# Expert rows gathered by slot tables from one-hot products, with part of the shared network and the numbering moved

## The chip, the cores and the metric

The kernel runs on one core of a Trainium2 chip. TensorE (PE) multiplies matrices, VectorE (DVE), ScalarE (ACT) and GpSimd (POOL) do elementwise work, SyncE (SP) issues most transfers. Each engine executes its own instructions in the order written, and semaphores tie the engines together. The metric is the device time of one execution in microseconds, as the median of several runs.

## The reference

Four blocks work in turn on `x`, 16 sequences of 128 tokens of 256 numbers (2048 tokens), each added to it behind a gate: a cross attention of 16 heads over all 2048 context rows, with numbers rounded to 8 bits; a mixture of 32 experts with a shared network; a WKV recurrence over each sequence; a mixture of 8 experts with a shared network. The change touches the second block:

```python
logits = x @ w_router
probs = jax.nn.softmax(logits.astype(jnp.float32), axis=-1)
w_topk, sel = jax.lax.top_k(probs, K)              # K = 4 of E = 32
...
pos = jnp.arange(T * K) - starts[sorted_e]
valid = pos < CAP                                   # CAP = 128 rows for each expert
buf = jnp.zeros((E, CAP + 1, Hq), x.dtype).at[sorted_e, dest].set(x[tok])
g = jnp.einsum('ech,ehf->ecf', buf, w_gate)         # 256 x 176
u = jnp.einsum('ech,ehf->ecf', buf, w_up)
y = jnp.einsum('ecf,efh->ech', jax.nn.silu(g) * u, w_down)
...
out = jnp.zeros((T, Hq), x.dtype).at[tok].add(gath * wv[:, None])
sh = jax.nn.silu(x @ sw_gate) * (x @ sw_up) @ sw_down   # 256 x 704
sh = jax.nn.sigmoid(x @ w_shared_gate) * sh
out = out + sh
```

A token's place within an expert is the number of earlier choices of that expert; places from 128 on are dropped.

## The kernel before

Tokens are handled as 16 tiles of 128, in NG = 4 groups of G = 4. The stages follow one another, with the head of each laid over the tail of the one before.

The attention (`attention_*`) fills about the first 750 us. In it SP writes zeros to the three tables of rows in device memory, one store of 512 rows with every fourth head (L433), beside the transposing transfers of the weights.

The front (`front_*`) comes next. For each group, DVE normalises the rows (`normalise`), PE turns them (`turn_rows`) and multiplies by the router (`router`, L1164), ACT copies the logits (L1232), DVE finds the four best experts, builds one-hot rows `hot` (L1306) and their sum `mask` (L1311) in `choose`, PE counts the places by products of the mask with a matrix of ones and a strictly triangular one (`places`, L1173 to L1177), and DVE's `place` (from L1318) turns counts into row numbers of the table `dispatched_rows` and closes the group with `destinations_ready`. `front_pool` then issues one indirect transfer for each tile and choice (L1142), 64 in all, each of which writes 128 rows (256 numbers, then the payload: experts, token numbers, weights) to their places in `dispatched_rows`. SP loads the shared weights and those of experts 0 to 9 (`load_expert`, L1048 to L1050; SLOTS = 10). The order of the work on each engine is written out by hand at the end of each `front_*` function.

The shared network is worked group by group. `hidden0(i, c0, c1)` is the hidden layer of group i in six chunks of 128 (the last of 64): PE makes the gate product (L1058, bank 0), ACT its silu (L1085), PE the up product (L1062, bank 1), and DVE multiplies them into `hT` (L1095). A gate product waits for the silu before, an up product for the multiplication before. `answers0(i)` is the down product of four tiles (L1075), each added to `x_sb` by DVE (L1103). Groups 0 and 1 stand at the end of the front, groups 2 and 3 in the mixing stage.

The experts (`experts_*`) follow. SP fetches the 128 rows of expert e from `dispatched_rows` (L1387) into one of RING = 6 buffers and loads the weights of expert e + 10 once expert e has been answered; PE turns the rows (L1409), multiplies by gate and up (L1418), turns the hidden layer (L1427) and multiplies by down (L1435), software-pipelined over three experts; ACT scales (L1457), takes silu (L1464) and weighs the answer into one of YRING = 4 buffers `yrow` (L1471); POOL scatters it to `answered_rows` by token and choice (L1529). DVE picks each row's target and weight out of the payload; `sum_payload(e)` (L1496) waits until the scatter of expert e - 4 has landed, and DVE's later work for e - 1 and e stands behind it.

The mixing stage (`mixing_*`) begins with the last expert. SP fetches the answered rows, and DVE adds them in `combine(g)` (L1959, then statistics L1946 and L1950). DVE's order begins: chunks 0 and 1 of group 2, `combine(0)`, chunks 2 and 3, `combine(1)`, chunks 4 and 5. PE's begins with all of `hidden0(2)` and `answers0(2)`. The second mixture, with its own tables and 39 blocks of rows (L2256 to L2283), ends the kernel.

## Time and profile before

| | |
|---|---|
| median of 3 runs | 1308.19 us (1306.60 to 1310.39) |
| the profiled execution, its own time | 1308.23 us |
| span of its trace, first to last instruction | 1306.4 us |
| busy: PE, DVE, ACT, POOL | 83%, 74%, 68%, 54% |
| attention | to about 750 us |
| front, groups 0 and 1 of the shared network | about 744 to 865 us |
| 32 experts | 865 to 961 us |
| mixing stage | 961 to 1179 us |
| second mixture | 1179 to 1306 us |

Times within the trace are microseconds from the start of its span. An engine's busy share over the whole span mixes stages with different limits, so each stage is read by itself: its windows, its waits, and the chain of work that ended last. PEclk is the granted TensorE clock as a share of 2.4 GHz.

### The profile page before, as it was taken

The page shows a single profiled execution, that of the slowest core. Times are in us where ns is not written, and L with a number is a line of the kernel's source. Part 1 is how long each engine was busy: PE and PEld are TensorE (multiplying, and loading weights), DVE is VectorE, ACT ScalarE, POOL GpSimd, SP SyncE. Part 2 cuts the span into 40 slices and gives each one's busy share as a digit, 9 for nine tenths or more (in the row PEclk, how much of TensorE's full clock was granted, in tenths as well). Part 3 has the DMA queues.
Part 4 walks back from the last instruction along what each step waited for, and adds up shares of the span by engine and source line. Part 5 has one row for each costly group of instructions (what it writes and reads, how often), then busy time and mean ns, then how long its engine had stood idle before and what let it go on. Part 6 is the DMA issues. An engine that isn't in the chain of part 4 may idle for free.

```text
span 1306.4 us, 23979 instructions
## 1 busy us (share of the span) xinstructions
PE 1086.5 (83%) x8185; PEld 634.8 (49%) x8300; DVE 962.8 (74%) x1787; ACT 893.6 (68%) x1533; POOL 702.6 (54%) x620
## 2 busy tenths in 40 slices
PE   6958888888888888888888768989988697798992
PEld 4623444444444444444444654556644254456771
DVE  6999899999999999999999564113345787642333
ACT  4649899999999999999999642124445466533441
POOL 3016988878888878887887437713330000452331
PEclk9969999999999999999999867989999898698997
DMA  5676788888888888888876391029853031123335
GB/s 172 126 140 140 152 171 160 162 175 166 166 184 160 160 181 166 167 180 163 161 149 106 58 278 60 19 58 275 257 190 133 1 82 51 42 83 92 100 95 208
DMA packets 393231, 182.50 MB, mean 140 GB/s; under 512 B 331376, under 2 KB 377045, under 8 KB 393112
## 3 DMA queue, kind: packets, MB, share of 16 engines
q1 hardware_dynamic: 384872, 164.30, 57.2%
q0 software_dynamic: 8016, 16.47, 3.6%
q8 instruction: 69, 1.13, 0.4%
q14 instruction: 50, 0.41, 0.1%
q10 hardware_dynamic: 224, 0.20, 0.1%
HBM read 52.70 MB, written 54.43 MB: 82 GB/s over the span
## 4 chain that ended last, share of the span: by engine, by line
PE 44%; DVE 31%; ACT 10%; issue 6%; DMA 5%; POOL 2%; SPq 1%; POOLq 0%; DVEq 0%; ACTq 0%
DVE top L368 20%; PE bank L217 8%; PE bank L231 7%; ACT weight L411 6%; PE bank L2267 4%; PE bank L1075 4%; PE bank L249 3%; DMA answered_rows<-yrow,target 3%; PE bank L1058 2%; PE bank L2283 2%; PE bank L1062 2%; PE bank L1435 2%; PE bank L1418 1%; PE bank L267 1%; DVE x_sb L1959 1%
## 5 line engine op out<-in xcount | busy, mean ns | idle before, releaser
L411 ACT ACTIVATE weight<-bank,bias,sq_all 128x1024 uint8<-128x1024 f32 x512 | 609.9, 1200 | 32.5 <-PE bank L231 27.1
L368 DVE TENSOR_REDUCE top<-bank 128x1 f32<-128x512 f32 (+1 forms) x683 | 610.8, 951 | 16.0 <-PE bank L217 4.7
L461 POOL CAST weight<-turned 128x2048 bf16<-128x2048 uint8 x256 | 478.8, 1892 | 43.5 <-PE bank L249 24.2
L231 PE MATMUL bank<-kT,query 128*128 128x512 bf16 x915 | 285.7, 384 | 26.3 <-ACT weight L411 12.1
L249 PEld LDWEIGHTS bank<-v_sb,weight 128*128 128x128 bf16 x4096 | 172.1, 97 | 109.8 <-POOL weight L461 7.5
L217 PE MATMUL bank<-kT,qspace 64*128 64x512 bf16 x687 | 138.2, 395 | 62.9 <-DVE top L368 62.9
L249 PE MATMUL bank<-v_sb,weight 128*128 128x16 bf16 x4096 | 172.7, 170 | 6.4 <-POOL weight L461 5.9
L217 PE MATMUL bank<-kT,query 128*128 128x512 bf16 x331 | 127.0, 384 | 2.1 <-DVE top L368 1.4
L1633 POOL DMA_INDIRECT dispatched_rows<-qspace,put x32 | 33.9, 1060 | 163.9 <-DVE qspace L2061 154.2
L231 PEld LDWEIGHTS bank<-kT,query 128*128 128x128 bf16 x1024 | 60.2, 97 | 104.2 <-ACT weight L411 60.9
L411 ACT ACTIVATION_READ_ACCUMULATOR weight<-bank,bias,sq_all 128x1 f32 x512 | 101.3, 198 | 0.0
L1142 POOL DMA_INDIRECT dispatched_rows<-qspace x64 | 64.0, 999 | 42.9 <-DVE qspace L1337 23.7
L217 PEld LDWEIGHTS bank<-kT,qspace 64*128 64x128 bf16 x687 | 33.4, 93 | 99.5 <-DVE top L368 94.3
L444 POOL TENSOR_TENSOR shift<-shift,nsq_all 128x4 f32<-128x4 f32 (+1 forms) x65 | 12.9, 198 | 127.9 <-DVE shift L372 127.9
L2388 POOL DMA_INDIRECT answered_rows<-yrow,target x39 | 37.9, 972 | 70.8 <-ACT yrow L2324 63.8
L1529 POOL DMA_INDIRECT answered_rows<-yrow,target x32 | 31.1, 972 | 81.2 <-ACT yrow L1471 76.4
L1085 ACT ACTIVATE sil<-bank 128x512 f32<-128x512 f32 (+1 forms) x24 | 14.3, 596 | 72.1 <-PE bank L1058 72.1
L217 PEld LDWEIGHTS bank<-kT,query 128*128 128x128 bf16 x337 | 32.7, 97 | 55.6 <-DVE top L368 36.4
L1058 PE MATMUL bank<-xT,sw 128*128 128x512 f32 (+1 forms) x96 | 49.3, 639 | 11.1 <-ACT sil L1085 10.3
L1095 DVE TENSOR_TENSOR hT<-sil,bank 128x512 f32<-128x512 f32 (+1 forms) x24 | 16.4, 682 | 57.2 <-PE bank L1062 49.4
L2359 DVE TENSOR_TENSOR eh<-esil,bank 128x176 f32<-128x176 f32 x39 | 13.2, 338 | 59.8 <-ACT esil L2317 59.8
L1062 PE MATMUL bank<-xT,sw 128*128 128x512 f32 (+1 forms) x96 | 47.4, 617 | 10.5 <-DVE hT L1095 10.5
(298 smaller groups left out, 1538.8 us busy)
## 6 DMA issues: line engine op xcount, KB each, us to landing
dispatched_rows<-zeros SPq DMA_DIRECT2D x32, 524.0 KB, 3.2
answered_rows<-zeros SPq DMA_DIRECT2D x16, 512.0 KB, 3.1
late<-answered_rows SPq DMA_DIRECT2D x16, 512.0 KB, 6.1
wgu<-in_L_ffn_w_gate SPq DMA_DIRECT2D x32, 176.0 KB
wgu<-in_L_ffn_w_up SPq DMA_DIRECT2D x32, 176.0 KB
wdn<-in_L_ffn_w_down SPq DMA_DIRECT2D x32, 176.0 KB
erow<-dispatched_rows SPq DMA_DIRECT2D x39, 131.0 KB, 2.1
dispatched_rows<-zeros SPq DMA_DIRECT2D x8, 536.0 KB, 3.1
```

The costliest lines, as they stand in the source:

```text
L217: pe.matmul(bank[:, k, :], q, kT[rows, h // 2, kb * 512:(kb + 1) * 512], start=True, stop=True).then_inc(s_blk, 1)
L231: mm = pe.matmul(unit[u % 2][:, v * 512:(v + 1) * 512], query2[:, t % 2, h, :], kT[:, h // 2, first + v * 512:first + (v + 1) * 512], star ...
L249: mm = pe.matmul(bank[:, 7, h * HD:(h + 1) * HD], weight[:, m % 3, r // 2, :, r % 2], v_sb[:, r, h * HD:(h + 1) * HD], start=(r == 0), sto ...
L368: ve.tensor_reduce(top[:, first:first + count], bank[:, first % 3:first % 3 + count, :], AX.X, ALU.max).then_inc(s_max, 1)
L411: ac.activation(weight8[:, n % BYTES, u * 1024:(u + 1) * 1024], unit[u], ACT.Exp, bias=bias[:, n:n + 1], scale=sq_all[:, n:n + 1], accum_o ...
L461: po.tensor_copy(weight[:, n % 3, :, :, :].rearrange("p c q two -> p (c q two)"), turned8[:, n % 3, :, :].rearrange("p c q -> p (c q)").bi ...
L1058: mm = pe.matmul(bank[0:w, 0, :], swg[:, k, c * P:c * P + w], xT[:, k, g * 512:(g + 1) * 512], start=k == 0, stop=k == CK - 1)
L1062: mm = pe.matmul(bank[0:w, 1, :], swu[:, k, c * P:c * P + w], xT[:, k, g * 512:(g + 1) * 512], start=k == 0, stop=k == CK - 1)
L1075: mm = pe.matmul(bank[:, 6 + k % 2, 0:C], hT[0:w, c, k * P:(k + 1) * P], swd[0:w, c, :], start=c == 0, stop=c == NW0 - 1)
L1142: po.indirect_dma_start(out=dispatched, out_offset=bass.IndirectOffsetOnAxis(ap=put[:, t, k:k + 1], axis=0), in_=rows0[:, t, :], in_offset ...
L2267: mm = pe.matmul(bank[:, 2 + b % 2, 0:2 * F1], erowT1[:, b % 2, k, :], w1gu[:, expert[b], k, :], start=k == 0, stop=k == CK - 1)
L2388: po.indirect_dma_start(out=answered1, out_offset=bass.IndirectOffsetOnAxis(ap=target1[:, b % YRING:b % YRING + 1], axis=0), in_=yrow1[:, ...
```

## The change

1. The 64 scatters are gone, and with them the table `dispatched_rows` and its zero stores (56 stores become 49 and a small one). SP instead stores each group's rows once, as they lie, to `kept_rows` (four stores). The remaining zero stores describe their table as partitions x 4 rows x row.
2. A table of sources is built: for each slot (0 to 127) of each expert, which row of `kept_rows` belongs there (row 0 to 127 of it are zeros). It comes from products of two one-hot arrays: `marked` (DVE, `mark_slots`, 128 x 16 x 128 in bf16: is this choice's place slot s?) and `numbered` (POOL, five `tensor_scalar` for each group: tile number and lane number at the chosen expert). PE's `fill_table(g)` adds 16 products for each group into bank 7; DVE's `take_table` turns the sums into row numbers. `marked` and `numbered` are single buffers, so that both wait for the products of the group before.
3. `place` loses two operations on 128 x 128 and a cast, and reads the counts from PSUM directly. `places` loses one product.
4. In the front, chunks 0, 1 and 2 of the shared network's group 0 are put between the routing steps, chunks 3 to 5 behind them.
5. Group 1 of the shared network moves to the head of the mixing stage, ahead of group 2; DVE does `combine(0)` between its hidden layer and its answers.
6. Expert rows are gathered by POOL with one indirect transfer for each expert, in the same queue as its scatters and six experts ahead. SP issues only weights.
7. SP loads three experts ahead of the routing and the other seven between the stores of the groups. The second mixture's fetches use other semaphores.

The diff, cut to its core:

```diff
@@ front_sync @@
-                for e in range(SLOTS):
+                for e in range(3):
                     load_expert(sp, e)
+                for g in range(NG):
+                    sp.wait_ge(sm_["destinations_ready"], g + 1)
+                    sp.dma_start(kept[P * (1 + g * G):P * (1 + (g + 1) * G), :].rearrange("(t p) c -> p t c", p=P),
+                                 rows0[:, g * G:(g + 1) * G, :]).then_inc(s_kept, 16)
+                    for e in range(3 + 2 * g, min(5 + 2 * g, SLOTS)):
+                        load_expert(sp, e)
@@ front_pool @@
-                    for t in tiles(g):
-                        for k in range(K0):
-                            po.indirect_dma_start(out=dispatched, ...).then_inc(s_scatter, 16)
+                    if g > 0:
+                        po.wait_ge(sm_["table_products"], g)
+                    for k in range(G):
+                        n = slice(k * K0, (k + 1) * K0)
+                        po.tensor_scalar(numbered[:, n, 0, :], hot[:, g % 2, n, :], float(g * G + k + 1), None, ALU.mult).then_inc(sm_["slots_numbered"], 1)
+                    po.tensor_scalar(numbered[:, :, 1, :], hot[:, g % 2, :, :], lane[:, 0:1], None, ALU.mult).then_inc(sm_["slots_numbered"], 1)
@@ front_tensor @@
+                def fill_table(g):
+                    pe.wait_ge(sm_["slots_numbered"], 4 + 5 * (g + 1))
+                    pe.wait_ge(sm_["slots_marked"], g + 1)
+                    if g == 0:
+                        pe.wait_ge(sm_["projections_added"], 2 * NG)
+                    for n in range(G * K0):
+                        mm = pe.matmul(bank[:, 7, 0:2 * E0], marked[:, n, :], numbered[:, n, :, :].rearrange("p a e -> p (a e)"),
+                                       start=g == 0 and n == 0, stop=g == NG - 1 and n == G * K0 - 1)
+                    mm.then_inc(sm_["table_products"], 1)
...
                 turn_rows(2)
+                pe.wait_ge(s_wf, 64)
+                hidden0(0, 0, 1)
                 places(1)
                 router(2)
                 turn_rows(3)
+                hidden0(0, 1, 2)
                 places(2)
+                fill_table(0)
                 router(3)
+                hidden0(0, 2, 3)
+                fill_table(1)
                 places(3)
-                pe.wait_ge(s_wf, 64)
-                hidden0(0, 0, 6)
+                fill_table(2)
+                fill_table(3)
+                hidden0(0, 3, 6)
+                pe.wait_ge(sm_["rows_chosen"], 1)
                 answers0(0)
-                hidden0(1, 0, 6)
-                answers0(1)
@@ front_scalar @@
                 copy_rows(2)
+                shared_scalar(ac, 0, 0, 1)
                 copy_logits(2)
                 exponentials(2)
                 copy_rows(3)
+                shared_scalar(ac, 0, 1, 2)
                 copy_logits(3)
                 exponentials(3)
+                shared_scalar(ac, 0, 2, 3)
                 residuals(3)
-                shared_scalar(ac, 0, 0, 6)
-                shared_scalar(ac, 1, 0, 6)
+                shared_scalar(ac, 0, 3, 6)
@@ front_vector @@
+                def mark_slots(g):
+                    if g == 0:
+                        ve.wait_ge(sm_["slots_numbered"], 4)
+                    else:
+                        ve.wait_ge(sm_["table_products"], g)
+                    at = slots[:, g * G * K0:(g + 1) * G * K0]
+                    ve.tensor_tensor(marked[:], slot_b[:].unsqueeze(1).broadcast_to([P, G * K0, P]),
+                                     at.unsqueeze(2).broadcast_to([P, G * K0, P]), ALU.is_equal).then_inc(sm_["slots_marked"], 1)
...
                 normalise(3)
+                mark_slots(0)
                 place(1)
+                hidden0(0, 0, 1)
                 choose(2)
+                mark_slots(1)
                 place(2)
+                hidden0(0, 1, 2)
                 choose(3)
+                mark_slots(2)
                 place(3)
-                hidden0(0, 0, 6)
+                mark_slots(3)
+                hidden0(0, 2, 5)
+                take_table()
+                hidden0(0, 5, 6)
                 answers0(0)
-                hidden0(1, 0, 6)
-                answers0(1)
@@ experts @@
-                def fetch_rows(sp, e):
+                def gather_rows(po, e):
...
+                    po.indirect_dma_start(out=erow[:, e % RING, :], out_offset=None, in_=kept,
+                                          in_offset=bass.IndirectOffsetOnAxis(ap=source[:, e:e + 1], axis=0), bounds_check=P + NTOK - 1,
+                                          oob_is_err=False).then_inc(s_er[e % RING], 16)
...
                 def experts_pool(po):
+                    po.wait_ge(s_kept, 16 * NG)
+                    po.wait_ge(s_zero, 16 * ZEROED)
+                    po.wait_ge(sm_["rows_chosen"], 1)
+                    for e in range(RING):
+                        gather_rows(po, e)
                     for e in range(E0):
+                        if e + RING < E0:
+                            gather_rows(po, e + RING)
                         po.wait_ge(sx_["targets_ready"], e + 1)
                         po.wait_ge(sx_["answers_weighted"], e + 1)
@@ mixing_tensor @@
                         pe.wait_ge(sx_["answers_weighted"], E0)
+                        for c in range(NW0):
+                            hidden0(1, c)
+                        for k in range(G):
+                            answers0(1, k)
                         for c in range(NW0):
                             hidden0(2, c)
@@ mixing_scalar @@
+                        shared_scalar(ac, 1, 0, NW0)
                         for c in range(4):
                             shared_scalar(ac, 2, c, c + 1)
@@ mixing_vector @@
+                        for c in range(NW0):
+                            hidden0(1, c)
+                        combine(0)
+                        for k in range(G):
+                            answers0(1, k)
                         hidden0(2, 0)
                         hidden0(2, 1)
-                        combine(0)
                         hidden0(2, 2)
                         hidden0(2, 3)
                         combine(1)
```

## Rows read from the trace of the kernel before

**Rows 1.** Windows: stretch, its length, busy us by engine, PEclk, DMA share, GB/s.

```profile
768.00:784.00 16.00, 6.11 (x33) 5.71 (x33) 13.32 (x65) 6.99 (x16) 12.47 (x12) 0.51 0.93 285
830.00:865.00 35.00, 33.87 (x100) 17.27 (x98) 6.29 (x11) 3.58 (x6) 16.46 (x17) 1.00 0.04 10
885.00:945.00 60.00, 54.98 (x243) 37.52 (x243) 19.35 (x102) 26.80 (x83) 19.43 (x20) 1.00 0.96 272
```

**Rows 2.** The chain that ended last, 784 to 890: start, us, what.

```profile
784.79 0.29 PE bank L1173
...
795.32 3.52 PE bank L1058 x4
...
818.94 12.00 PE bank L1075 x48
...
867.65 0.68 PE bank L1409 x2
```

**Rows 3.** Timeline of the routing, DVE and PE: start, us, instruction, idle before it.

```profile
775.30 1.03 DVE L1311 TENSOR_REDUCE qspace<-qspace 128x128 bf16<-128x512 f32 x1
...
776.72 1.43 DVE L1285 TENSOR_SCALAR qspace<-x_sb,rec,nm 128x256 f32<-128x256 f32 x4
...
778.08 0.28 DVE L1318 TENSOR_TENSOR qspace<-bank,limit 128x128 f32<-128x128 f32 x1
...
781.07 0.47 DVE L1293 MAX8 qspace<-qspace 128x8 f32<-128x32 f32 x4
```

**Rows 4.** Nearest prices: page's groups, groups by form, one line, then the timeline.

```profile
L461 POOL CAST weight<-turned 128x2048 bf16<-128x2048 uint8 x256 | 478.8, 1892 | 43.5 <-PE bank L249 24.2
...
L1959 DVE TENSOR_TENSOR x_sb<-x_sb,late 128x1024 f32<-128x1024 f32 x16 | 19.6, 1224 | 3.1 <-DMA late<-answered_rows 2.7
...
L1005 POOL TENSOR_SCALAR wp<-wp,vscale x2: 922/922/922, 87.2 to 88.1; 128x256 f32<-128x256 f32 x2
...
12.21 0.37 POOL L994 TENSOR_SCALAR token_f<-token_f 128x64 f32<-128x64 f32 x1
...
793.57 1.65 PE L1176 MATMUL bank<-qspace,every 128*128 128x128 bf16 x15
```

**Rows 5.** Timeline, two POOL casts beside DVE additions that end at 977.62.

```profile
975.14 2.48 DVE L1959 TENSOR_TENSOR x_sb<-x_sb,late 128x1024 f32<-128x1024 f32 x2
...
976.81 0.86 POOL L1617 CAST kind<-kind_i 128x8 f32<-128x8 uint32 x1
...
977.78 0.20 POOL L1619 CAST qspace<-place_i 128x32 f32<-128x32 uint32 x1
```

**Rows 6.** Timeline at the head of the mixing stage.

```profile
980.10 3.65 PE L1062 MATMUL bank<-xT,sw 128*128 128x512 f32 x4 [5.80 <-DVE hT L1095]
...
994.71 6.03 PE L1075 MATMUL bank<-sw,hT 128*128 128x256 f32 x24 [0.84 <-DVE hT L1095]
```

**Rows 7.** Timeline, first products of the experts.

```profile
869.02 2.71 PE L1418 MATMUL bank<-wgu,qspace 128*128 128x352 f32 x4 [0.29 <-ACT qspace L1457]
...
874.72 1.35 PE L1418 MATMUL bank<-wgu,qspace 128*128 128x352 f32 x4
```

**Rows 8.** Timeline of POOL's scatters, and one line's longest.

```profile
878.51 0.97 POOL L1529 DMA_INDIRECT answered_rows<-yrow,target  x1 [27.16 <-ACT yrow L1471]
...
881.00 0.97 POOL L1529 DMA_INDIRECT answered_rows<-yrow,target  x1 [1.52 <-ACT yrow L1471]
...
962.70 0.97 POOL L1529 DMA_INDIRECT answered_rows<-yrow,target  x1 [0.30 <-issue]
...
L1633 POOL DMA_INDIRECT dispatched_rows<-qspace,put x32: 972/972/2446, 1111.2 to 1175.9; - x32
```

**Rows 9.** Landing of indirect transfers: L1142 in 768 to 772, L1529 in 885 to 895.

```profile
DMA to landing us min/median/max: 5.6/5.8/6.0
...
DMA to landing us min/median/max: 6.1/6.1/6.1
```

**Rows 10.** DMA issues of the page: one of an expert's three loads of weights.

```profile
wgu<-in_L_ffn_w_gate SPq DMA_DIRECT2D x32, 176.0 KB
```

More of the change, by code:

```diff
@@ L46, in program @@
     ROW = C + 3 * K0
-    dispatched = nc.dram_tensor("dispatched_rows", [E0 * CAP, ROW], F32).ap()
+    kept = nc.dram_tensor("kept_rows", [P + NTOK, ROW], F32).ap()
     answered = nc.dram_tensor("answered_rows", [NTOK * K0, C], F32).ap()
@@ L53, in program @@
     answered1 = nc.dram_tensor("answered_rows_1", [NTOK * K1, C], F32).ap()
[L54 removed]
+    ZEROED = (NTOK * K0 + E1 * NTOK) // 512 + 1
     HUGE, TINY = 1e18, 2.0 ** -60
@@ L87, in program @@
         s_wp, s_g = sem("projection_weights_loaded"), sem("gates_loaded")
-        s_zero = sem("dispatched_rows_zeroed")
+        s_zero = sem("tables_zeroed")
         xr = x.rearrange("t p c -> p t c")
@@ L420, in attention_sync @@
             def attention_sync(sp):
-                stores = [(table, width, r) for table, width in ((dispatched, ROW), (answered, C), (dispatched1, ROW1))
-                          for r in range(table.shape[0] // 512)]
+                stores = [(table[512 * r:512 * (r + 1), :].rearrange("(p f) c -> p f c", p=P), width)
+                          for table, width in ((answered, C), (dispatched1, ROW1)) for r in range(table.shape[0] // 512)]
                 for n in range(NHEAD):
@@ L430, in attention_sync @@
                         pad_queries(sp, t + 1)
+                    if n == 8:
+                        sp.dma_start(kept[0:P, :], zeros[:, 0:ROW]).then_inc(s_zero, 16)
                     if n >= 8 and n % 4 == 0 and n // 4 - 2 < len(stores):
-                        table, width, r = stores[n // 4 - 2]
-                        sp.dma_start(table[512 * r:512 * (r + 1), :].rearrange("(p f) c -> p (f c)", p=P), zeros[:, 0:4 * width]).then_inc(s_zero, 16)
+                        cleared, width = stores[n // 4 - 2]
+                        sp.dma_start(cleared, zeros[:, 0:4 * width].rearrange("p (f c) -> p f c", f=4)).then_inc(s_zero, 16)
                     sp.wait_ge(s_exp, 2 * n + 2)
@@ L1039, in program, with rows1_fetched @@
             s_er = [sem(f"x0_rows_fetched_{s}") for s in range(RING)]
+            s_er1 = s_ew[0:RING]
+            def rows1_fetched(b):
+                weights = 48 * len(range(b % RING, E0, SLOTS))
+                return weights + 16 * (b // RING + 1)
             s_es = [sem(f"x0_answers_scattered_{s}") for s in range(YRING)]
@@ L1119, in program @@
             mask = carve(NT * E0 // 2).bitcast(BF16).rearrange("p (t e) -> p t e", e=E0)
-            ge, slot = carve(G * E0).rearrange("p (t e) -> p t e", e=E0), carve(2 * G * E0).rearrange("p (b t e) -> p b t e", b=2, e=E0)
-            destf, put = carve(NT * K0), carve(NT * K0).bitcast(U32).rearrange("p (t k) -> p t k", k=K0)
+            slots = carve(NT * K0 // 2).bitcast(BF16)
             total, share = carve(NT), carve(NT)
+            table = buffers(first_experts)
+            marked = late[:, 6, :].bitcast(BF16).rearrange("p (n s) -> p n s", s=P)
+            numbered = late[:, 7, 0:G * K0 * E0].bitcast(BF16).rearrange("p (n a e) -> p n a e", a=2, e=E0)
+            slot_b, slot_n, lane, lane_n = table("slot_b", [P, P], BF16), table("slot_n", [P, P], U32), table("lane", [P, 1]), table("lane_n", [P, 1], U32)
+            tile_f, source = table("tile_f", [P, E0]), table("source", [P, E0], U32)
             def front_sync(sp):
@@ L1172, in places @@
                     at = bank[:, 3, 0:G * E0]
-                    pe.matmul(at, every[:], number[:].unsqueeze(1).broadcast_to([P, G, E0]), start=True, stop=False)
+                    pe.matmul(at, before[:], mask[:, g * G:(g + 1) * G, :], start=True, stop=False)
                     for t in range(g * G + G - 1):
                         first = max(t + 1 - g * G, 0)
-                        pe.matmul(at[:, first * E0:], every[:], mask[:, t:t + 1, :].broadcast_to([P, G - first, E0]), start=False, stop=False)
-                    pe.matmul(at, before[:], mask[:, g * G:(g + 1) * G, :], start=False, stop=True).then_inc(sm_["places_counted"], 1)
+                        mm = pe.matmul(at[:, first * E0:], every[:], mask[:, t:t + 1, :].broadcast_to([P, G - first, E0]), start=False,
+                                       stop=t == g * G + G - 2)
+                    mm.then_inc(sm_["places_counted"], 1)
+                def fill_table(g):
[7 more added lines that the diff above has]
+                    mm.then_inc(sm_["table_products"], 1)
                 def hidden0(i, c0, c1):
@@ L1305, in choose @@
                     settle()
+                    if g >= 2:
+                        ve.wait_ge(sm_["slots_numbered"], 4 + 5 * (g - 1))
                     step(ve.tensor_tensor(hot[:, g % 2, :, :].rearrange("p (t k) e -> p t k e", k=K0),
@@ L1330, in place @@
                     step(ve.reciprocal(sgate[:, s], sgate[:, s]))
-                    step(ve.tensor_reduce(destf[:, g * G * K0:(g + 1) * G * K0], picked[:], AX.X, ALU.add))
+                    with nc.allow_low_precision(reason="whole numbers, compared with those below 128"):
+                        step(ve.tensor_reduce(slots[:, g * G * K0:(g + 1) * G * K0], picked[:], AX.X, ALU.add))
                     settle()
```

59 lines of the change are left out of this document (26 added, 33 removed).

## The prediction

> **What bounds the kernel now.** I read the windows by stage first. While groups are routed (768 to 784), PE is busy 6.1 of 16 us at the lower clock of 1.2 GHz and DVE 13.3: DVE's steps set the time, PE has room. From 830 to 865 PE is busy 33.9 of 35 us with group 1 of the shared network, at 2.4 GHz, and before that with group 0. From 885 to 945 the DMA engines are 96% busy at 272 GB/s [rows 1]. The chain of waits says the same: routing ends at 795.32 with the first chunk, the answers of group 0 start at 818.94, and the first expert's rows are turned at 867.65, right behind group 1 [rows 2]. POOL's 64 scatters are in none of these: they end before the shared network does. Removing them gives nothing by itself. What counts is when the experts can start, what each costs, and what the moved group costs later.
>
> **Routing and tables, worked on the axis of the trace before.** Without its two operations on 128 x 128 (0.28 us) and the cast, `place` takes 2.5 us instead of 3.0 (778.08 to the next `choose` at 781.07) [rows 3]. So the second mask, which ended at 776.33, is ready at 775.8, and the last `normalise` ends at 777.7 (776.72 + 1.43, less 0.5) [rows 3].
>
> Unseen before is the marking of slots, 128 x 2048 in bf16 with one operand repeated along the row. The nearest row is an addition of 128 x 1024 at 1.22 us [rows 4]; twice that, less one fixed part, is 2.3. The lower bound is 1.2, if bf16 goes at double rate. I take 2.3: the reduction into bf16 (1.03 us for 512 elements [rows 3]) shows no gain from the type. POOL's numbering is four operations of 128 elements and one of 512. From 0.37 us for 64 and 0.92 for 256 [rows 4] I get 0.55 each and 1.7, so 3.9 us for a group; the bounds are 2.0 (at the rate of the 1.89 us cast of 2048 [rows 4], with five fixed parts) and 5. Sixteen products of the table cost 1.6 us at 1.2 GHz by fifteen at 1.65 [rows 4], 0.9 at 2.4 GHz.
>
> Marking and numbering of one group are released together, by the products of the group before. A POOL cast of 8 elements took 0.86 us, to 977.67, while DVE's addition of two SBUF operands ran to 977.62; a larger one behind it took 0.20 [rows 5]. So I let them follow each other: 6.2 us, not 3.9. The Trainium skill says this too (SBUF — State Buffer, "SBUF: two separate sides"): a DVE operation with two SBUF inputs and a GpSimd operation that reads SBUF exclude each other for the whole instruction. It speaks against the numbering on GpSimd, and the row above agrees with it; without exclusion the sum below would be 4.6 us smaller.
>
> DVE in order from 777.7: mark 780.0, place 782.5, multiply chunk 0 (0.7) 783.2, choose (3.7, from 781.07 to the count at 784.79 [rows 2, 3]) 786.9. PE counts and fills table 0 to 788.7. DVE marks to 791.0, places to 793.5, multiplies chunk 1 to 794.2, chooses to 797.9. PE's up product of chunk 2 waits for that multiplication; with table 1 it ends at 797.1. ACT's three silus and their table loads fit between DVE's steps. Then the single buffers bind: POOL wakes in 0.6, mark and numbering take 6.2, so table 2 can start at 803.9 and ends at 805.5 (at 1.2 GHz, as the product behind an idle 5.8 us at 980.10 [rows 6]); DVE marks group 3 to 807.8, POOL numbers to 811.7, PE fills to 813.3. Three chunks are left. Six took from 795.32 to 818.94, the first slow [rows 2]: three take about 13.2 us, so the answers start at 826.5, not 818.94. They take 12.0, and the experts start 0.6 behind, at **839.1** against 867.65: **-28.5 us**. The three chunks moved into the routing hide about 10 us of PE work, and the table takes that and 7.6 more. The source table is ready near 821.5 and six gathers need 6 x 1.27 us of POOL and a landing, so they hide behind the answers. The stores of `kept_rows` (0.5 MB each, in 768 to 813) and the seven later weight loads land long before 839; the load that fills the DMA in 768 to 784 [rows 1] is only thinned.
>
> **Experts.** The fetch latency is already in that start. PE now comes from full work: the first products of a pair of experts took 2.7 and 2.5 us against 1.35 later [rows 7]; **-2.7 us**. POOL has two indirect transfers for each expert. Back to back one costs 0.97 + 0.30 [rows 8], so 2.54 for both, against the 2.49 at which experts follow one another when nothing waits (878.51, 881.00) [rows 8]. If POOL must wake for each answer, it is 0.8 + 0.97 + 0.30 + 0.97 = 3.04. But from 878.51 to 962.70 the 31 steps took 84.2 us, 2.72 each [rows 8], since in the busy stretch scatters land after 6.1 us [rows 9] and the ring of four holds DVE. A gather in the same queue could lengthen that. Against it: 1.28 us apart, as dense as gather and scatter will be, L1142's scatters landed in 5.6 to 6.0 us with the DMA as full [rows 9]. Bytes per expert stay (528 KB of weights [rows 10], 134 in, 131 out), and at 272 GB/s [rows 1] they need 2.9 us whoever issues them. I take **+1.0 us**, bounds -3 and +9 (3.04 for the 26 steps with a gather against their present share).
>
> **Mixing.** Group 1 comes first. PE starts at 961.45 as now; six chunks end by 983.6 (five at 3.44 and a first one behind ACT's table load). `combine(0)` takes 6.8 us (four additions of 1.22 [rows 4], then statistics), to 990.4; its rows landed long before. Answers run beside it, but the third waits for DVE's first addition: end 997.0. Chunks 0 to 3 of group 2 end at 1010.8, `combine(1)` runs 1011.5 to 1018.3, chunk 4's multiplication to 1019.0, chunk 5 to 1021.5. Now group 2's answers start at 994.71, after an idle 5.8 us that also cost a product at 3.65 instead of 1.88 [rows 6]. **+26.8 us** for 34 us of moved work. Behind this point every engine's order is the same and the fetches have more slack.
>
> **Other edits.** Seven fewer zero stores, in smaller pieces, lie beside a stretch that DVE bounds; new semaphores and a product less: 0, bounds -1 and +2.
>
> **Sum.** -28.5 - 2.7 + 1.0 + 26.8 = -3.4 us on the profiled execution's 1308.23 (span 1306.4), which is the median within 0.1: **1304.8 us**.
>
> **Rivals.**
> - The tables are quick: marking and numbering run side by side (4.6 less) and PE stays at 2.4 GHz or marking is at double rate: -8 to -14, at 1300 to 1294; worked as 1299. For it: PE has more work in the routing. Against it: [rows 5].
> - Slower: POOL becomes the bound of the experts. A gather, never seen here, may cost more than a scatter; the longest indirect transfer took 2.45 us [rows 8]. With the whole gather at 1.8 us, POOL needs 0.97 + 0.30 + 1.8 + 0.30 = 3.37 for each of 26 steps: 26 x 3.37 + 5 x 2.49 = 100.1 against 84.2, +16 in place of +1: 1320. At 1.3 us (2.87) it only cancels the gain; it turns to slower by 0.3% at about 1.5. Against it: the scatters of 1072 and 1024 bytes cost the same 0.97.
> - It doesn't do what it says: the interleaved chunks delay DVE's routing as much as they hide. The main case has this nearly so. If additionally POOL pays its waking (3.04) at each expert, 1311: no change.
>
> **How the numbers follow.** Main case 0.45, its own range 1301 to 1309; quick tables 0.25; nothing gained 0.13; POOL bound 0.17. The range 1293 to 1317 takes in the quick case and half of the slow one. About 0.3% (3.9 us) is what a measurement can tell: faster means below 1304.3, which is nearly half of the main case and the quick one, 0.46; slower, above 1312.1, 0.19; between them 0.35.
>
> **What would show it.** In the changed kernel: marking at 2.3 us, POOL's five operations at 3.9 us and stretched beside marking; two PE gaps of about 5 us ahead of tables 2 and 3; the answers of group 0 starting near 826 and the first turn of expert rows near 839; POOL's pairs 2.54 us apart and weighed answers 2.7 apart; scatters landing in about 6 us; answers of group 2 some 60 us behind the last expert instead of 33. Wrong would be: gathers over 1.3 us, a wait of PE for gathered rows, or an attention that ends elsewhere than before.

## The result, and the profile after

The changed kernel takes **1299.33 us** (median of 4 runs, 1298.18 to 1300.09) against 1308.57 for the kernel before on the same chip: a ratio of 0.9933, with a 95% interval of 0.9918 to 0.9949. It is faster by 0.67%. The forecast was 1304.8, in a range of 1293 to 1317. The profiled execution took 1299.77 us, with a span of 1298.0 where the kernel before had 1306.4.

The windows of the changed kernel, over the stretches of [rows 1]:

```profile
core 0: us, PE busy (x) PEld busy (x) DVE busy (x) ACT busy (x) POOL busy (x), PEclk, DMA share, GB/s
768.00:784.00 16.00, 10.44 (x43) 7.55 (x42) 13.36 (x59) 8.90 (x16) 2.65 (x4) 0.79 0.38 113
830.00:865.00 35.00, 32.98 (x150) 22.57 (x149) 10.60 (x53) 14.80 (x46) 16.92 (x17) 1.00 0.61 176
885.00:945.00 60.00, 56.76 (x219) 34.75 (x217) 16.79 (x80) 25.32 (x66) 28.14 (x30) 1.00 0.67 214
```

DVE is as busy in the routing as it was (13.4 of 16 us); PE went from 6.1 to 10.4, part of it at 2.4 GHz, and the DMA engines from full to 38%. From 836 on, where group 1 of the shared network stood, experts are at work. The chain of waits of the changed kernel has these pieces, where [rows 2] had 795.32, 818.94 and 867.65:

```profile
796.90 2.49 POOL late L1166
800.11 1.57 POOL late L1167
801.73 1.05 PE bank L1209 x16
802.93 2.56 POOL late L1166
...
807.40 1.57 POOL late L1167
809.02 1.04 PE bank L1209 x16
810.05 3.49 PE bank L1064 x4
...
823.17 11.98 PE bank L1081 x48
...
835.71 0.46 PE bank L1466 x2
...
924.83 1.88 PE bank L1492 x8
...
987.83 6.03 PE bank L1081 x24
```

From 796 to 810 the chain runs through POOL's numbering (L1166, L1167) and the table products (L1209). Then come the shared chunks, the answers of group 0 at 823.17, the first turn of expert rows at 835.71, the last down product at 924.83, and the answers of group 2 at 987.83. The account of the two spans:

| stage | before | after | difference | forecast |
|---|---|---|---|---|
| start to the first expert turn | 867.65 | 835.71 | -31.9 | -28.5 |
| first turn to the last weighed answer | 93.75 | 91.5 | -2.3 | -1.7 |
| from there to the answers of group 2 | 33.3 | 60.6 | +27.3 | +26.8 |
| the rest | 311.7 | 310.2 | -1.5 | 0 |
| span | 1306.4 | 1298.0 | -8.4 | -3.4 |

The attention ends at the same time in both. The last weighed answer ends at 961.40 and 927.21 us.

### The profile page after: what moved, and what is told of

The parts are those of the page before. It is cut to its first block, busy times and chain, and to the rows that moved or that the text cites. A ratio compares the mean times of both kernels' runs of the same rounds, so it can differ in the third digit from the quotient of the medians.

```text
span 1298.0 us, 24037 instructions
## 1 busy us (share of the span) xinstructions
PE 1081.6 (83%) x8245; PEld 631.3 (49%) x8360; DVE 969.6 (75%) x1781; ACT 899.4 (69%) x1537; POOL 696.8 (54%) x610
## 4 chain that ended last, share of the span: by engine, by line
PE 42%; DVE 31%; ACT 10%; issue 7%; DMA 5%; POOL 4%; SPq 1%; POOLq 0%; DVEq 0%; ACTq 0%
DVE top L368 20%; PE bank L217 7%; PE bank L231 7%; ACT weight L411 6%; PE bank L2340 4%; PE bank L1081 3%; DMA answered_rows<-yrow,target 3%; PE bank L249 3%; PE bank L1064 3%; PE bank L2356 2%; PE bank L1068 2%; PE bank L1721 1%; PE bank L267 1%; DVE x_sb L2028 1%; POOL weight L463 1%
## 5 line engine op out<-in xcount | busy, mean ns | idle before, releaser
L411 ACT ACTIVATE weight<-bank,bias,sq_all 128x1024 uint8<-128x1024 f32 x512 | 610.0, 1200 | 32.4 <-PE bank L231 27.2
L231 PEld LDWEIGHTS bank<-kT,query 128*128 128x128 bf16 x1024 | 60.1, 97 | 104.2 <-ACT weight L411 60.6
L2461 POOL DMA_INDIRECT answered_rows<-yrow,target x39 | 37.9, 972 | 69.5 <-ACT yrow L2397 54.9
L2340 PE MATMUL bank<-late,erowT 128*128 x156 | 53.8, 468 | 0.0
L1081 PE MATMUL bank<-sw,hT 128*128 128x256 f32 x192 | 47.9, 393 | 4.6 <-DVE hT L1101 2.5
L1068 PE MATMUL bank<-xT,sw 128*128 128x512 f32 (+1 forms) x96 | 45.6, 597 | 4.7 <-DVE hT L1101 4.7
```

The costliest lines, as they stand in the source:

```text
L231: mm = pe.matmul(unit[u % 2][:, v * 512:(v + 1) * 512], query2[:, t % 2, h, :], kT[:, h // 2, first + v * 512:first + (v + 1) * 512], star ...
L411: ac.activation(weight8[:, n % BYTES, u * 1024:(u + 1) * 1024], unit[u], ACT.Exp, bias=bias[:, n:n + 1], scale=sq_all[:, n:n + 1], accum_o ...
L1068: mm = pe.matmul(bank[0:w, 1, :], swu[:, k, c * P:c * P + w], xT[:, k, g * 512:(g + 1) * 512], start=k == 0, stop=k == CK - 1)
L1081: mm = pe.matmul(bank[:, 6 + k % 2, 0:C], hT[0:w, c, k * P:(k + 1) * P], swd[0:w, c, :], start=c == 0, stop=c == NW0 - 1)
L2340: mm = pe.matmul(bank[:, 2 + b % 2, 0:2 * F1], erowT1[:, b % 2, k, :], w1gu[:, expert[b], k, :], start=k == 0, stop=k == CK - 1)
L2461: po.indirect_dma_start(out=answered1, out_offset=bass.IndirectOffsetOnAxis(ap=target1[:, b % YRING:b % YRING + 1], axis=0), in_=yrow1[:, ...
```

## Experiments

Each ratio is to the kernel before on the same chip. Where the routing starts varies by up to 2 us between traces of these kernels; so, where it matters, times are counted from the start of the first marking (777.68 in the changed kernel, where chunk 3 starts 32.4 us later and the answers of group 0 45.5 later).

### Group 1 back in front of the experts

```diff
@@ front @@
                 answers0(0)
+                hidden0(1, 0, 6)
+                answers0(1)
@@ mixing_tensor @@
-                        for c in range(NW0):
-                            hidden0(1, c)
-                        for k in range(G):
-                            answers0(1, k)
```

> The changed kernel (1299.3 us, profiled span 1298.0) with group 1 of the shared network put back behind group 0, ahead of the experts; tables, gathers and interleaving stay. My theory: the front takes 33.9 us more (first expert turned near 869.6 instead of 835.7), the mixing stage's head 27.3 us less (group 2's answers 33.3 us behind the last expert instead of 60.6): 1299.3 + 33.9 - 27.3 = 1305.9 us. Rival: the move is worth nothing because its work is hidden nowhere, and the gain comes from tables and gathers alone: 1299 us or less.

Measured: 1305.13 us, ratio 0.9974 (0.9958 to 0.9990). Its chain has the answers of group 1 right ahead of the experts:

```profile
822.07 11.97 PE bank L1081 x48
...
855.82 12.01 PE bank L1081 x48
...
868.40 0.46 PE bank L1471 x2
```

The theory had 1305.9 us; the rival's 1299 is out. Tables, gathers and interleaving without the move leave the experts' first turn where [rows 2] has it (868.40 for 867.65), and the answers of group 2 start at 994.26 for 994.71. What is left, a quarter of a per cent, is clear of the noise in the times, but in the traces it lies behind that point: 309.9 us for 311.7. In the traces of the other runs whose kernel before takes 1308 us, this stretch is between 308.4 and 311.7 us, with either kernel, so I count none of it as the change's; its cause is not shown.

### The kernel before with group 1 moved

```diff
@@ kernel before, front @@
                 answers0(0)
-                hidden0(1, 0, 6)
-                answers0(1)
@@ mixing_tensor @@
+                        for c in range(NW0):
+                            hidden0(1, c)
+                        for k in range(G):
+                            answers0(1, k)
                         for c in range(NW0):
                             hidden0(2, c)
```

> The kernel before (1308.6 us) with only group 1 of the shared network moved to the mixing stage; the 64 scatters stay. My theory: the scatters, which ended hidden at 852 and landed at 854, now stand on the path: rows are fetched from 854 and turned at 856.6, only 11.1 us earlier than 867.65, while the mixing stage's head costs 27.3 more: 1324.8 us. Rival: scatters do not bound, the experts start at 833.5: 1308.6 - 34.1 + 27.3 = 1301.8 us.

Measured: 1320.14 us, ratio 1.0090 (1.0057 to 1.0122). Now the scatters end last:

```profile
848.28 2.15 DMA dispatched_rows<-qspace
850.44 2.10 DMA qspace<-dispatched_rows
...
852.67 0.68 PE bank L1404 x2
```

Some fifty of the 64 scatters are pieces of this chain, 1.28 us apart. The move alone costs 12 us: the experts win 15 us (867.65 to 852.67) and the mixing stage gives back 27. The forecast of the run was 4.7 too high: the rows had been landed and fetched by 852.67, not 856.6, and 2.1 of these 3.9 us are a first scatter that went out sooner than in the trace of before (766.07 for 768.18). So "removing the scatters gives nothing by itself" holds only with group 1 in front. Together with the move, what takes their place is worth the difference of this run's first turn to 835.71: 17 us, and 19 if this run's sooner start is taken off.

### All six chunks behind the tables

```diff
@@ front, on PE, ACT and DVE @@
-                hidden0(0, 0, 1)
                 places(1)
...
-                hidden0(0, 1, 2)
...
-                hidden0(0, 2, 3)
...
-                hidden0(0, 3, 6)
+                hidden0(0, 0, 6)
```

> The changed kernel with all six chunks of group 0 behind the last table product, none between the routing steps. My theory: the chain of numberings on POOL (each about 6.6 us beside the marking) sets the end of the tables, at 811 instead of 810, and all six chunks follow, the first at 1.2 GHz: answers of group 0 near 834.9 instead of 823.2, 1311.0 us. Rival: the interleaved chunks delay the routing as much as they hide: 1299 to 1302 us.

Measured: 1308.26 us, ratio 1.0001 (0.9986 to 1.0017). Its chain (POOL's four small operations left out):

```profile
805.96 1.57 POOL late L1167
...
807.58 1.04 PE bank L1209 x16
808.62 3.57 PE bank L1064 x4
...
832.25 11.98 PE bank L1081 x48
```

Counted from the first marking (776.78 here), the first chunk starts 31.8 us later, chunk 3 of the changed kernel 32.4: without the chunks between its steps the routing is only 0.5 us shorter. The answers start 55.5 us after it for 45.5, so 10.0 later, and by the ratios the time is 9 us longer. The interleaving is worth 9 to 10 us, and without it the whole change is worth nothing (forecast of the run: 1311.0 us). The rival in which the chunks delay as much as they hide is out.

### Numbering behind marking

```diff
@@ front_pool @@
                     if g > 0:
                         po.wait_ge(sm_["table_products"], g)
+                        po.wait_ge(sm_["slots_marked"], g + 1)
```

> The changed kernel with one wait more: POOL numbers a group only once DVE has marked it. If DVE's marking and POOL's numbering exclude each other, they take turns anyway: numbering takes 3.7 us behind 2.3 of marking, each of groups 2 and 3 ends 1 to 2 us later through the wake-up and the later start, first product of chunk 3 near 811.5 to 812 instead of 810.05: 1301 us. If POOL's operations are merely slower beside DVE, or its 2.5 us operation has another cause, they stay at 6.0 us behind the marking and groups 2 and 3 end 4.6 us later: 1304 us.

Measured: 1300.55 us, ratio 0.9939 (0.9917 to 0.9960): no slower than the changed kernel's 0.9933. Timelines of DVE's marking and of POOL, of group 2 and 3, in the changed kernel:

```profile
796.72 2.28 DVE L1386 TENSOR_TENSOR late<-slot_b,qspace 128x2048 bf16<-128x2048 bf16 x1
802.80 2.29 DVE L1386 TENSOR_TENSOR late<-slot_b,qspace 128x2048 bf16<-128x2048 bf16 x1 [1.41 <-PE bank L1209]
795.68 4.33 POOL L1166 TENSOR_SCALAR late<-qspace 128x128 bf16<-128x128 f32 x4 [1.83 <-PE bank L1209]
800.11 1.56 POOL L1167 TENSOR_SCALAR late<-qspace,lane 128x512 bf16<-128x512 f32 x1
802.93 4.38 POOL L1166 TENSOR_SCALAR late<-qspace 128x128 bf16<-128x128 f32 x4 [1.25 <-PE bank L1209]
807.40 1.56 POOL L1167 TENSOR_SCALAR late<-qspace,lane 128x512 bf16<-128x512 f32 x1
```

and with the wait, group 2, where POOL started only after the marking had ended:

```profile
796.03 2.28 DVE L1387 TENSOR_TENSOR late<-slot_b,qspace 128x2048 bf16<-128x2048 bf16 x1
798.49 2.39 POOL L1167 TENSOR_SCALAR late<-qspace 128x128 bf16<-128x128 f32 x4 [4.51 <-DVE late L1387]
800.98 1.56 POOL L1168 TENSOR_SCALAR late<-qspace,lane 128x512 bf16<-128x512 f32 x1
```

Four operations take 2.39 us alone and 4.3 beside the marking. In the chain above it is one of the four that takes 2.49 or 2.56 us in place of 0.53: it stands for the length of the marking. Group 3 is the clean case, since its marking and numbering are released together: forced one after the other, its table starts 6.5 us behind the start of the marking (803.67 to 810.20) instead of 6.2 (802.80 to 809.02), because they had followed each other anyway. The rival is out: operations that are merely slower beside DVE would have kept the numbering at 6 us behind the marking, and it takes 3.95 (2.39 and 1.56). Counted from the first marking, chunk 3 starts 34.7 us later for 32.4; 2.0 of that has come about by the table of group 2, where in the changed kernel POOL had done two of its operations before the marking began. The Trainium skill's rule (SBUF — State Buffer, "SBUF: two separate sides"), by which a DVE operation with two SBUF inputs and a GpSimd operation that reads SBUF exclude each other, is what these rows show.

### Numbering on ScalarE, two buffers, and another order

Four kernels: ScalarE's numbering alone; two buffers alone; both; both and another order of the work.

```diff
@@ front_scalar (and taken from front_pool) @@
+                    for k in range(G):
+                        ac.activation(numbered[:, n, 0, :], hot[:, g % 2, n, :], ACT.Copy, scale=float(g * G + k + 1))
+                    ac.activation(numbered[:, :, 1, :], hot[:, g % 2, :, :], ACT.Copy, scale=lane[:, 0:1])
@@ two buffers: POOL or ACT, and DVE @@
-                    if g > 0:
-                        po.wait_ge(sm_["table_products"], g)
+                    if g > 1:
+                        po.wait_ge(sm_["table_products"], g - 1)
@@ order on PE (and so on DVE and ACT) @@
                 places(3)
+                hidden0(0, 3, 4)
                 fill_table(2)
+                hidden0(0, 4, 5)
                 fill_table(3)
-                hidden0(0, 3, 6)
+                hidden0(0, 5, 6)
```

> The changed kernel with the numbering taken from GpSimd to ScalarE (five scaled copies for each group), each copy waiting as before for the table products of the group before it; GpSimd does nothing in the routing steps. Theory (the gaps of TensorE ahead of the table products of groups 2 and 3 are the numbering: 3.7 us alone, about 6.1 us beside marking, because GpSimd stands while VectorE reads two operands): ScalarE isn't held up by VectorE, so marking (2.3 us) and numbering (five copies, estimated at 0.3 to 0.6 us each) run side by side and take about 3 us; chunk 3 of the shared expert starts at about 804 us instead of 810.05 and the time is about 1293.5 us (-5.9). Rival (the gaps are single buffers: marking itself can't begin before the table products of the group before it): marking and numbering still start at the same moment, chunk 3 starts no more than 2 us earlier and the time is 1297.5 us or more.

> The changed kernel with two buffers each for the marked and the numbered one-hot rows, so that marking and numbering of a group wait for the table products of the group before the last; numbering stays on GpSimd. Theory (GpSimd's numbering held up by VectorE's marking is what ends last): GpSimd still can't number before the destinations of the group are known, and these come last, so chunk 3 starts within 1 us of 810.05 and the time is about 1298.5 us. Rival (the buffer is what ends last): the two gaps of TensorE of about 6 us each shrink and the time is about 1293 us.

> Two buffers and numbering on ScalarE together. If GpSimd's numbering alone bounds, this gives what ScalarE's numbering alone gives (about 1293 us) and the buffers add nothing; if both bound, it is lower than either alone, near 1290 us.

> Two buffers, numbering on ScalarE, and another order on TensorE: chunk 3 of the shared expert's first group ahead of the table products of group 2 and chunk 4 ahead of those of group 3, so that a product lies in each of the two gaps of about 6 us. Theory (the gaps of TensorE ahead of table products of groups 2 and 3, 795.6 to 801.7 us and 802.8 to 809.0 us, are all that is left to fill): the answers of group 0 start near 811.5 us instead of 823.2, the experts' first turn moves by the same 11.6 us, and the time is about 1288 us. Rival (the gather of the first expert's rows, which can't start before the tables are read out and written, ends last instead): the first turn moves by 6 us at most and the time is 1293 us or more.

On ScalarE the copies wait for the choices of their group and not, as on POOL, for its places too. These four ran on a chip where the kernel before took 1361.17 us, and the changed kernel was not run there, so their times stand only beside one another. They were 1315.11, 1316.24, 1311.64 and 1305.20 us; ratios 0.9660 (0.9643 to 0.9678), 0.9663 (0.9649 to 0.9677), 0.9633 (0.9620 to 0.9646) and 0.9587 (0.9570 to 0.9604). The front can be compared with the changed kernel's by their traces, counted from the first marking, since one kernel has nearly the same front on both chips: the last of the four has 18.3 and 31.0 again in the trace of its second run below, and the changed kernel 33.1 and 45.6.

| | chunk 3 starts | answers of group 0 start |
|---|---|---|
| changed kernel | 32.4 | 45.5 |
| two buffers | 29.3 | 42.0 |
| ScalarE | 27.3 | 40.9 |
| both | 25.2 | 38.6 |
| both and order | 18.3 | 31.0 |

With two buffers, numbering of group 3 still meets its marking, since both now start when the places are known (timelines of POOL with two buffers; group 2, then group 3):

```profile
791.16 2.38 POOL L1166 TENSOR_SCALAR late<-qspace 128x128 bf16<-128x128 f32 x4 [4.34 <-DVE qspace L1377]
...
799.86 4.32 POOL L1166 TENSOR_SCALAR late<-qspace 128x128 bf16<-128x128 f32 x4 [4.31 <-DVE qspace L1377]
```

and on ScalarE five copies take 1.5 us right beside the marking (timelines of DVE and ACT, single buffers, group 2):

```profile
795.23 2.28 DVE L1393 TENSOR_TENSOR late<-slot_b,qspace 128x2048 bf16<-128x2048 bf16 x1
795.61 0.90 ACT L1284 ACTIVATE late<-qspace 128x128 bf16<-128x128 f32 x4
796.41 0.71 ACT L1285 ACTIVATE late<-qspace,lane 128x512 bf16<-128x512 f32 x1
```

So neither pure theory holds. On chunk 3, taking the numbering from GpSimd is worth 5 us (expected: 6) and the second buffers 3 (expected: less than 1), together 7; part of the 7 can be the earlier release of ScalarE's copies, which no run takes apart. In the last kernel a chunk stands ahead of each late table, and PE's timeline (from its second run) has no gap left until the answers wait for the table:

```profile
795.80 1.96 PE L1064 MATMUL bank<-xT,sw 128*128 128x512 f32 x4
797.60 1.88 PE L1068 MATMUL bank<-xT,sw 128*128 128x512 f32 x4
799.31 0.63 PE L1201 MATMUL bank<-late 128*128 128x64 bf16 x16
799.78 1.96 PE L1064 MATMUL bank<-xT,sw 128*128 128x512 f32 x4
801.58 1.88 PE L1068 MATMUL bank<-xT,sw 128*128 128x512 f32 x4
803.56 0.63 PE L1201 MATMUL bank<-late 128*128 128x64 bf16 x16
```

### The changed kernel and the new order on one chip

> The changed kernel itself, as the base for the runs with ScalarE's numbering and two buffers, which were made on a chip on which the kernel before took 1361.2 us and not 1308. On such a chip the first expert's turn of those runs (830.6 us with ScalarE's numbering against 835.7 here) gives about 1320 us for it, a ratio to the kernel before of 0.970; on a chip where the kernel before takes 1308 us it takes 1299 us. If the gain of ScalarE's numbering were nothing, it would take 1315 us on the first kind of chip.

> Two buffers, numbering on ScalarE and the other order once more, beside the changed kernel on one chip. Its first turn was at 821.1 us against 835.7, so it should be 10 to 15 us faster than the changed kernel on the same chip: about 1287 us where the kernel before takes 1308 us, about 1305 us where it takes 1361 us. Rival: what is won in front of the experts is lost in the experts' stage, because the weights of experts 10 to 31 come no sooner; then it is less than 8 us faster.

No edit to either. Measured, beside a kernel before of 1308.58 us: the changed kernel 1297.72 (1296.39 to 1299.72; ratio 0.9930, 0.9902 to 0.9957), the new order **1283.60** (1281.46 to 1284.83; ratio 0.9813, 0.9786 to 0.9841). It beats both kernels: 14.1 us off the changed one, within the 10 to 15 expected. It is the front: the first gate product of the experts starts at 822.36 against 835.06 in the trace, which is 44.7 against 59.3 us behind the first marking, and the experts' stage no longer than before (89.8 us to the end of the last down product, against 90.6), so the rival is out. What was expected of the changed kernel on the chip with 1361 us (a ratio of 0.970) stays untested.

### The kernel before without the weights of experts 10 to 31

```diff
@@ kernel before, experts_sync @@
-                        if e + SLOTS < E0:
-                            sp.wait_ge(sx_["answers"], e + 1)
-                            load_expert(sp, e + SLOTS)
```

> The kernel before, with the weights of experts 10 to 31 of the first mixture not loaded (their turns run with the weights of the first ten, so this part of the computation is changed). Theory (the experts' stage is bound by TensorE's turns of 2.49 us, and what the stage takes beyond that is stalls behind the transfers): the 31 turns take 31 x 2.49 = 77.2 us instead of 83.7, and where the kernel before takes 1308 us this takes about 1302 us (1355 us where that takes 1361). Rival: the stalls are not the weight transfers' doing and the time stays within 2 us of the kernel before. Its trace also shows the scatters in front of the first group on this chip: where the kernel before takes 1361 us, the theory that the scatters' transfers fall behind their issue says that the first turn comes 40 us or more later than at 867.65 us.

Measured: 1296.27 us, ratio 0.9912 (0.9885 to 0.9938). The loads cost the kernel before 12 us, twice the 6 expected. The scatters L1526 of this run, which are L1529 of the kernel before (in 885 to 895 they landed in 6.1 us, [rows 9]):

```profile
L1526 POOL DMA_INDIRECT answered_rows<-yrow,target x32: 971/971/975, 877.1 to 951.6; - x32
DMA to landing us min/median/max: 2.2/2.4/3.2
```

The 31 steps take 74.5 us (877.1 to 951.6), not 84.2, which is 9.7 of the 12. In the kernel before, DVE's `sum_payload` waited 41.3 us in 22 places for scatters to land; here nothing waits for them, and the first 25 steps take 2.49 us each (877.09 to 939.34). So the mechanism expected is right, what holds the turns above 2.49 us is the landing under the load of the weights, and the size missed, in part because the last six steps are quicker than 2.49. The other 2.6 of the 12 us lie outside the steps, and no run isolates them. In the changed kernel the trace has the same waits (84.7 us for the 31 steps, 37.7 us of waits in 22 places). But there POOL's pair of 2.66 us would stand in place of the 2.49, and no run took the loads from that kernel. The question of this run about the chip with 1361 us stays open, since the run was made beside a kernel before of 1308.58 us.

### A longer turn on GpSimd

```diff
@@ changed kernel, experts_pool @@
                         if e + RING < E0:
+                            po.iota(slot_n[:], ...)
+                            po.iota(slot_n[:], ...)
                             gather_rows(po, e + RING)
```

> The changed kernel with two more small GpSimd operations (an iota over 128 x 128, estimated at 0.5 us with its wait) ahead of each gather of the experts' stage. It prices the point from which GpSimd decides. Theory (GpSimd's pair of gather and scatter, 2.65 us a turn, is just below the stage's mean turn of 84.3 / 31 = 2.72 us): each further us on the pair comes out whole, the turn grows to about 3.2 to 3.6 us and the time by 10 to 25 us. Rival (GpSimd has room, what bounds are transfers and TensorE): the time grows by less than 3 us.

Measured: 1317.44 us, ratio 1.0072 (1.0044 to 1.0100), 19.7 above the changed kernel on the same chip. POOL, the first turns:

```profile
848.31 1.03 POOL L1448 DMA_INDIRECT qspace<-kept_rows,source  x1 [0.77 <-POOL slot_n L1592]
849.65 1.02 POOL L1597 DMA_INDIRECT answered_rows<-yrow,target  x1 [0.31 <-issue]
850.69 0.25 POOL L1590 IOTA slot_n<- 128x128 uint32 x1
851.01 0.23 POOL L1592 IOTA slot_n<- 128x128 uint32 x1
852.02 1.03 POOL L1448 DMA_INDIRECT qspace<-kept_rows,source  x1 [0.77 <-DVE target L1557]
```

A turn is 3.70 us on POOL instead of 2.66, and this is the pace of the first 25 turns (scatters from 842.2 to 934.80). Without the iotas these 25 turns took 73.5 us in the trace of the same chip (842.01 to 915.47), 2.94 each, and the last six 11.9. So POOL had 0.28 us of room in a mean turn (2.94 - 2.66), and what goes beyond it came out whole: 25 x (3.70 - 2.94) = 19. The premise that the turns take 2.72 was a mean with a fast end in it.

## Why the prediction was right, and where it missed

The direction and the range were right. The mechanisms are those of the likeliest case, but the time is 5.5 us below its value and 1.7 below its own range (1301 to 1309). The gain is 9.2 us, where the sum had 3.4. That was less than the 3.9 us that the forecast called measurable, and it gave faster a chance of only 0.46, so that the direction came out clearly is not to its credit. Step by step:

- **The sum's large terms.** -28.5 was -31.9, and +26.8 was +27.3. The run with group 1 in front and the run of before with it moved show that neither half wins much alone (0.9974 and 1.0090): the moved 34 us of work cost 27 in mixing, and only without the scatters do the experts start early enough to pay for that.
- **Marking and numbering** were right in size: 2.29 us for 2.3, and 2.39 + 1.56 = 3.95 for 3.9; 6.2 beside each other by the chain (from 795.68 to 801.67 is 6.0). The gaps of PE ahead of tables 2 and 3 were there, 3.9 and 6.3 us of idle time.
- **The mis-sized term is the table product.** I took 1.6 us for sixteen at 1.2 GHz and 0.9 at 2.4, from fifteen products of 128 columns (1.65 [rows 4]). These have 64 columns: 1.04 and 0.49 us. Over four tables that is up to 2 of the 3.2 us by which chunk 3 came earlier (810.05 for 813.3), and the experts' first turn, 835.71 for 839.1, came earlier by no more than this. The rest is DVE's routing steps (`choose` took 3.4 us for 3.7, `place` 2.3 for 2.5) and POOL's wake-up behind table 1, which took 0.14 us (795.54 to 795.68) for 0.6. PE's clock is little of it: the forecast had tables 2 and 3 at 1.2 GHz, and there they were. Windows of the changed kernel, for the clock:

```profile
784.00:800.00 16.00, 10.13 (x89) 6.25 (x87) 14.22 (x42) 9.08 (x14) 9.81 (x9) 0.99 0.68 191
800.00:815.00 15.00, 7.02 (x40) 3.98 (x41) 4.21 (x8) 0.60 (x1) 7.28 (x7) 0.56 0.24 73
```

  From 784 to 800 the granted clock is 2.4 GHz (0.99; the kernel before had 0.53 there), after a stretch in which PE was 10.4 of 16 us busy instead of 6.1. Behind the two gaps it falls back to 1.2 GHz (0.56), and chunk 3 pays for it (3.49 us for a gate product that takes 1.72 at full clock). In the second run of the changed kernel PE's first chunk in the routing was still at 1.2 GHz (3.62 us for its gate product, where this trace has 2.23). Chunk 3 then started 0.7 us later behind the first marking, and the answers of group 0 at the same place, 45.6 us for 45.5.
- **The gather** costs 1.02 us, and beside gathers a scatter does too instead of 0.97, so the pair is 2.66 and not 2.54. The stage lost 0.5 us over its 31 steps, forecast 1.0. The first experts came 2.8 us quicker (2.7 forecast), from PE at 2.4 GHz. One thing that the forecast would have called wrong did show, in a small size: PE waited for gathered rows, 0.8 us in two places, and its weight loads 4.0 us in eight.
- **The rest**, forecast 0, was -1.5. In the second mixture one group of products took 1.18 us where it had taken 2.24 at the lower clock (chains at 1178.72 and 1186.28); no run isolates this, and it lies within what the traces of this stretch differ by.
- **Quick tables** (0.25): the time, 1299.3, is that of this rival, but its mechanism isn't. Marking and numbering exclude each other, as the run with the wait shows. Only its second half, PE at 2.4 GHz in the routing, came true, and only up to about 800 us.
- **POOL becomes the bound** (0.17): not here. The price was put at a turn of 2.72; the run with iotas puts the room at 0.28 us a turn. By that estimate a gather of 1.3 us would have been free, one of 1.5 would cost 25 x 0.2 = 5, and one of 1.8 would cost 25 x 0.5 = 12.5, not 15.
- **Nothing hidden** (0.13): the six chunks behind the tables give 1.0001. The interleaving hides the about 10 us that was claimed (10.0 in the trace, 9 in the time).

## What to carry to other kernels

Moving work behind a stage pays only if the stage's other inputs are there by then: price the move alone and the removal alone; here the removal alone gave 0.3% and the move alone cost 0.9%. When a chain runs through two engines whose operations exclude each other, give one half to a third engine, and put independent products in front of the wait that is left; here that was worth more (14 us) than the change itself (9 us). Before calling an engine nearly bound, take the turn's length from the stretch where it has its full work, not from a mean over the stage.

## What the runs showed that was not expected

- **One GpSimd operation stands for a whole VectorE operation.** 0.53 us became 2.49 and 2.56 beside a comparison with two SBUF inputs of 2.29 us. Right after it, POOL's next operations beside DVE's shorter ones took 0.53 and 1.57 us again, as alone. With two buffers, where the larger one met other work of DVE, it took 1.92 in two of four groups. ScalarE's copies took as long beside the comparison as away from it (0.90 and 0.91 us for four).
- **The same kernel took 22 us longer on another chip, by stalls in two places.** The kernel with the new order took 1283.60 us on one chip and 1305.20 on another, where the kernel before went from 1308.58 to 1361.17. By the two traces, 8.3 us of it are in the experts' stage and 13.6 between its end and the second mixture's experts. There ScalarE stood 17 us behind a table load, 14 of them with its operand ready, until POOL had issued its last scatter (at 1161.03):

```profile
1144.45 1.28 ACT L1944 ACT_TABLE_LOAD   x1
1162.98 0.60 ACT L1944 ACTIVATE sil<-bank 128x512 f32<-128x512 f32 x1 [17.25 <-remote]
```

  On the other chip the same instruction stood 3.39 us, for its product. The three other kernels of that chip have the same stall (17.8, 17.9 and 18.6 us), and each of the four ends 2.0 to 3.7 us behind the start of the last scatter. That the kernel before, with 64 more scatters, loses 53 us there would fit, but no trace of it was taken on that chip; what holds ScalarE is open.
- **Scatters land in 2.4 us without the load of the weights and in 5.1 under it** (medians over the 32 scatters, in the kernel before; 6.1 at most). From 885 to 945 us the DMA engines were 31% busy in the one and 96% in the other. A buffer ring that looks deep enough by the first number stalls by the second.
